# Graph layers: in the three weighted passes the weight table becomes the stationary operand and the features the moving one

## The chip, the cores and the metric

The kernel runs on one core of a Trainium2 chip. The metric is the device time of one launch in microseconds (us). The kernel before was timed three times: 2389.75, 2402.13 and 2397.53 us, median 2397.53 us.

## The reference, cut to what matters

A graph of 3125 nodes with 96 features and 103125 edges goes through four blocks. What this change touches is the second one, three GCN convolutions with edge weights:

```python
norm = dis[src_a] * w_a * dis[dst_a]
h = x @ W
msg = h[src_a] * norm[:, None]
out = jax.ops.segment_sum(msg, dst_a, num_segments=n)
return out + b
```

It is called three times, with a relu after the first and the second. After the third comes `layernorm(x + ...)`. The block before it (a mean over neighbours) and the one after it (two convolutions without weights, with a norm over the nodes) have the same shape of sum, with counts of edges in place of weights; an attention over the edges ends the network.

## The kernel before, in words

**Tables.** A first stage (`add_edges`) turns the list of edges into two dense tables of 3125 x 3125: how many edges go from one node to another (bf16) and the sum of their weights (f32). Each is stored in 25 blocks, one for each group of 125 target nodes (LANES = L = 125, NT = 25). A block holds 25 pieces of 125 source nodes x 125 target nodes.

**Passes and jobs.** `graph_layers` multiplies features by these tables. It has 6 passes (k = 0 to 5) of 25 jobs each, job j = 25 k + b making the sums of target group b. Passes 1, 2 and 3 are the weighted ones (`WEIGHTED`); they read `w_tab`, a ring of four slots of 1562.5 KB that SyncE's queue (SP) refills when the job four before it is done (`acc_done`). The other passes read the counts, `c_tab`, with the features split in three bf16 pieces side by side (288 columns).

**A job on TensorE.** In `main` (L1264) a job is 25 matmuls, t = 0 to 24, which add up in one PSUM bank, `acc[j % 2]`. In a count job the count block is stationary and the features stream (L1285): sums come out with the nodes on the partitions. In a weighted job the features of source group t, `g` (125 x 96), are stationary and the 125 x 125 piece of the weights streams (L1273): sums come out turned, 96 features on the partitions and 125 nodes in the free dimension. All of it is f32, and each f32 matmul shows as two instructions in the profile, with a weight load each.

**What follows a job.** The sums have to be multiplied by the layer's 96x96 weight, for which they must stand turned (features on partitions) in SBUF, in `aggT`. In a count job VectorE adds the three pieces into `h` (`sums`, L1390), TensorE turns `h` through `turn` (`turned`, L1225), and ScalarE copies the result into `aggT` (L1168). In a weighted job the sums are turned already, and ScalarE copies them from `acc` (L1165). Then TensorE makes the product (`product`, L1233), and VectorE ends the job (`finish`, L1434): scale, bias, relu, scale into the next pass's `g` (L1444, L1447), or in pass 3 the residual, a layer norm (`normalise`, L1418) and the split in bf16 pieces (L1453 to L1459). In pass 3 TensorE also turns x (`x_turn`, L1255) at place 21 of the following job.

**Order.** The order on each engine is written out by hand. TensorE puts the turn and the product of job j - 1 among the matmuls of job j, after matmul t = `at[0]` and t = `at[1]` (L1302). Where job j is weighted, that is (6, 10); after a weighted job there is only the product, at place 6. VectorE's loop over the weighted jobs (L1562) calls `finish(j)` and nothing else. `acc` has two banks: job j waits until the sums of job j - 2 have been read (L1290 to L1294). In the first job of a pass TensorE waits before each matmul for its piece of the last pass's result (`g_ready`, L1272; `g3_ready`, L1281).

Of the kernel before, what the change touches and what calls it, by code (L numbers as in the profile page):

```python
# [26 lines left out]
D = 96  # L27
# [3 lines left out]
NT = -(-N // P)  # L31
# [847 lines left out]
def graph_layers(nc, w_blocks, c_blocks, weights, rows, columns, kvq_w, kvq_b, kv_dram, q3_dram, ident, ci, x, eps, last_stored,  # L879
# [12 lines left out]
    with ctx:  # L892
# [120 lines left out]
        def c_index(j):  # L1013

            return j if j < NT else j - 3 * NT
# [96 lines left out]
        def _(act):  # L1112
# [45 lines left out]
            for k in range(PASSES):  # L1158
                for b in range(NT):
                    j = k * NT + b  # L1160
                    if k == 0:
                        own_rows(b)
                    if k in WEIGHTED:
                        act.wait_ge(acc_done, j + 1)
                        nc.scalar.copy(aggT[j % 2][0:D], acc[j % 2][0:D, 0:L]).then_inc(agg_ready, 1)  # L1165
                    else:
                        act.wait_ge(h_turned, c_index(j) + 1)
                        nc.scalar.copy(aggT[j % 2][0:D], turn[j % 2][0:D, 0:L]).then_inc(agg_ready, 1)  # L1168
                    if k == 0:
                        if b > 0:  # L1170
                            deviation(b - 1)
                        if b == W_DEG_AT:
                            act.wait_ge(dis_max, 1)
                            nc.scalar.activation(dis[:], dis[:], ACT.Sqrt).then_inc(dis_sqrt, 1)
                        if b > W_DEG_AT:
                            for late in range(min(5 * (b - W_DEG_AT - 1), b - 3), b - 2 if b == NT - 1 else min(5 * (b - W_DEG_AT), b - 2)):
                                first_g(late)
                        if b == NT - 1:
                            deviation(b)
                            for late in range(b - 2, NT):  # L1180
                                first_g(late)
                    elif k == 3:
                        act.wait_ge(var_ready, NT + b + 1)
                        nc.scalar.activation(sd[:], mv[:, 1:2], ACT.Sqrt, bias=eps[:, 0:1]).then_inc(sd_ready, 1)
                        act.wait_ge(x_turned, b + 1)
                        nc.scalar.copy(feat[1][:, nodes(b)], turn[j % 2][0:D, 0:L]).then_inc(feat_ready, 1)
                    elif k > 3:
                        act.wait_ge(prod_done, j + 1)
                        nc.scalar.copy(feat[k % 2][:, nodes(b)], prod[j % 2][0:D, 0:L]).then_inc(prod_copied, 1)
                if k > 3:  # L1190
                    i = k - 4
                    act.wait_ge(gvar_ready, i + 1)
                    nc.scalar.activation(gs[:, 1:2], gs[:, 0:1], ACT.Sqrt, bias=eps[0:D, 1:2]).then_inc(gsd_ready, 1)
                    act.wait_ge(gscale_ready, i + 1)

                    def relu(c):
                        area = slice(c * PB * L, (c + 1) * PB * L)
                        nc.scalar.activation(feat[k % 2][:, area], feat[k % 2][:, area], ACT.Relu, bias=gs[:, 4:5],
                                             scale=gs[:, 3:4]).then_inc(relu_ready, 1)

                    relu(0)
                    relu(1)
                    for c in range(CHUNKS):
                        if c + 2 < CHUNKS:
                            relu(c + 2)
                        if k == 4:
                            act.wait_ge(hT_turned, c + 1)
                            split(CHUNKS + c, turn[c % 2][0:L, 0:PB * D].rearrange("p (j d) -> p j d", d=D))
                            split_on(CHUNKS + c)
                        else:  # L1210
                            act.wait_ge(var5_ready, c + 1)
                            nc.scalar.activation(sd5[:], var5[:], ACT.Sqrt, bias=eps[:, 0:1]).then_inc(sd5_ready, 1)
                            act.wait_ge(shift5_ready, c + 1)
                            for u in range(PB):
                                done = nc.scalar.activation(x[0:L, PB * c + u, :], y5[c % 2][0:L, u, :], ACT.Identity,
                                                            bias=shift5[0:L, u:u + 1], scale=sd5[0:L, u:u + 1])
                            done.then_inc(out_ready, 1)
                            if c > 0:
                                out_copies(c - 1)
                            xT_copy(c)  # L1220
# [3 lines left out]
        def _(pe):  # L1224
            def turned(j):  # L1225

                if count_job(j):
                    pe.wait_ge(h_ready, c_index(j) + 1)
                    if 4 * NT <= j < 4 * NT + 2:
                        pe.wait_ge(feat_ready, NT - 1 + j % NT)  # L1230
                    nc.tensor.transpose(turn[j % 2][0:D, 0:L], h[j % 2][0:L, :], ident[0:L, 0:L]).then_inc(h_turned, 1)

            def product(j):  # L1233

# [29 lines left out]
            def main(j, t):  # L1264

                k, b = divmod(j, NT)
                if k in WEIGHTED:
# [2 lines left out]
                        pe.wait_ge(w_landed[s], 16 * (w_index(j) // W_SLOTS + 1))  # L1270
                    if b == 0:
                        pe.wait_ge(g_ready, (k - 1) * NT + t + 1)  # L1272
                    return nc.tensor.matmul(acc[j % 2][0:D, 0:L], g[(k - 1) % 2][0:L, t, :], w_tab[s][0:L, t, :], start=t == 0, stop=t == NT - 1)  # L1273
                s = c_index(j) % C_SLOTS
                if t == 0:
                    pe.wait_ge(c_landed[s], 16 * (c_index(j) // C_SLOTS + 1))
# [11 lines left out]
            for j in range(JOBS):  # L1288
                k, b = divmod(j, NT)
                if j >= 2:  # L1290
                    if count_job(j - 2):
                        pe.wait_ge(sums_read, c_index(j - 2) + 1)
                    else:
                        pe.wait_ge(agg_ready, j - 2 + 1)  # L1294
                for t in range(NT):
                    last = main(j, t)
                    if t == NT - 1:
# [1 line left out]
                    if j == W_DEG_AT and t == 23:  # L1299
                        pe.wait_ge(wsum_ready, W_SUM_PARTS)  # L1300
                        nc.tensor.transpose(deg[1][0:L, 0:NT], wsum[:], ident[0:NT, 0:NT]).then_inc(w_deg_ps, 1)
                    at = (6, 10) if not count_job(j) else (11, 19) if k == 0 else (8, 16)  # L1302
                    fresh = b == 0 and k in (4, 5)
                    if j >= 1 and not (b == 0 and k == 5):
                        if t == at[0] and count_job(j - 1):
                            turned(j - 1)
                        if t == at[1 if count_job(j - 1) else 0]:
                            product(j - 1)
                        if t == 21:
                            x_turn(j - 1)  # L1310
# [49 lines left out]
        def _(dve):  # L1360
# [29 lines left out]
            def sums(j):  # L1390

                b = j % NT
                dve.wait_ge(acc_done, j + 1)
                if c_index(j) >= 2:
                    dve.wait_ge(h_turned, c_index(j) - 1)
                pieces = acc[j % 2][0:L, 0:D3].rearrange("p (k c) -> p c k", k=3)
                if j < NT:
                    in_degree = acc[j % 2][0:L, D3:D3 + 1]
# [161 lines left out]
                    degrees()  # L1560
            finish(NT - 1)
            for j in range(NT, 4 * NT):  # L1562
                finish(j)
                dve.drain()
            for i in range(2):
                first = (4 + i) * NT
                sums(first)
# [1438 lines left out]
```

## Time and profile before

| | |
|---|---|
| median of three runs | 2397.53 us |
| span of the profiled execution | 2394.0 us |
| three weighted passes, 670 to 1090 us | 420 us, clock 1.00 |
| attention, from 1360 us on | 1034 us, clock 0.50 |

Of the profiled execution the profile has the span, first to last instruction; the median lies 3.5 us above it. PE is TensorE's matmuls, PEld its weight loads, DVE VectorE, ACT ScalarE, POOL GpSimd, SP the queue of SyncE. A row of a group gives the line, engine, operation, tiles (out<-in), shapes and count, then busy us and mean ns of one, then the idle time of the engine just before. `125*96 125x125` on a matmul says: stationary operand 125 rows x 96 columns, moving operand 125 x 125. A matmul's recorded duration holds its latency, so in a stream the distance between starts is shorter than the duration. The clock is the one granted to TensorE, 1.00 for 2.4 GHz and 0.50 for 1.2 GHz.

### The profile page before, as it was taken

Reading aid. Unit: us, or ns where it says so; the run is one execution under the profiler, and the core shown is the slowest. Engines: PE = TensorE matmul, PEld = TensorE weight load, DVE = VectorE, ACT = ScalarE, POOL = GpSimd, SP = SyncE. Lnnn points to the kernel's source line nnn. Section 1 sums busy time; section 2 is a strip of 40 time slices with the busy share of each in tenths; the row PEclk is TensorE's granted clock in tenths of the full one; section 3 lists DMA queues with packets and bytes.
Section 4 is the critical chain, followed back from the end, with each engine's and each line's share of the span. In section 5 each row is a group of like instructions: output and inputs, shape, how many; then the busy total and the mean of one; then the engine's idle time right before and its main releaser. Section 6 shows DMA issues by size and latency. Waiting matters only on the chain. (4 is left out here: it accounts for less than half of the span.)

```text
span 2394.0 us, 46888 instructions
## 1 busy us (share of the span) xinstructions
PE 1970.0 (82%) x14784; PEld 1716.6 (72%) x14785; DVE 1371.8 (57%) x3363; ACT 999.8 (42%) x2697; POOL 954.4 (40%) x947
## 2 busy tenths in 40 slices
PE   7888888887999999999898477777777777777775
PEld 3666666665799999998786367676767676776765
DVE  6999999997720111442324455555555555555554
ACT  5788888885320000111213334343434343434432
POOL 3122222222000000000001477777777777777775
PEclk9999999998999999999998555555555555555555
DMA  1477766768888887785562575565555555555552
GB/s 55 82 110 129 114 115 110 127 117 197 265 312 288 293 290 285 284 297 192 179 226 87 153 183 162 159 166 155 162 162 161 161 159 163 160 162 156 160 158 64
DMA packets 225379, 416.45 MB, mean 174 GB/s; under 512 B 130818, under 2 KB 150296, under 8 KB 215448
## 3 DMA queue, kind: packets, MB, share of 16 engines
q1 hardware_dynamic: 186414, 334.76, 50.1%
q0 software_dynamic: 38784, 79.48, 12.7%
q8 instruction: 88, 1.44, 0.2%
q14 instruction: 93, 0.76, 0.1%
HBM read 347.71 MB, written 66.43 MB: 173 GB/s over the span
## 5 line engine op out<-in xcount | busy, mean ns | idle before, releaser
L2354 POOL DMA_INDIRECT attention_windowed_vkv<-kv_dram,ttention_windowed_vsrc x808 | 781.1, 967 | 247.0 <-issue 222.5
L2445 PE MATMUL attention_windowed_vps_e<-attention_windowed_vwe,attention_windowed_vattr 97*128 97x96 f32 x1616 | 403.7, 431 | 119.9 <-DVE ttention_windowed_vscore L2520 90.7
L2459 PE MATMUL attention_windowed_vps_s<-attention_windowed_hot,attention_windowed_vmsg 128*104 128x32 f32 x1616 | 319.8, 362 | 177.4 <-DVE attention_windowed_vmsg L2524 153.4
L2445 PEld LDWEIGHTS attention_windowed_vps_e<-attention_windowed_vwe,attention_windowed_vattr 97*128 97x128 f32 x1616 | 366.5, 332 | 125.6 <-issue 125.6
L2459 PEld LDWEIGHTS attention_windowed_vps_s<-attention_windowed_hot,attention_windowed_vmsg 128*104 128x104 f32 x1616 | 297.4, 289 | 208.9 <-DVE attention_windowed_vmsg L2524 180.1
L1273 PE MATMUL graph_layers_acc<-graph_layers_w_tab,graph_layers_g 125*96 125x125 f32 x3750 | 417.8, 269 | 0.0
L678 ACT ACTIVATE add_edges_hot_lo<-add_edges_hot_lo,parts 128x128 bf16<-128x128 bf16 x1212 | 371.4, 387 | 90.1 <-DVE add_edges_hot_lo L761 90.1
L1273 PEld LDWEIGHTS graph_layers_acc<-graph_layers_w_tab,graph_layers_g 125*96 125x96 f32 x3750 | 406.6, 163 | 0.1
L729 PE MATMUL add_edges_ps_four<-add_edges_hot,add_edges_hot_lo 128*128 128x200 bf16 x2424 | 332.0, 258 | 0.0
L1103 POOL CAST graph_layers_g<-graph_layers_w_tab 125x480 bf16<-125x480 f32 x4 | 2.3, 585 | 736.0 <-ACT graph_layers_w_tab L1150 730.0
L2387 ACT ACTIVATE attention_windowed_vmsg<-ttention_windowed_vscore 128x32 f32<-128x32 f32 x202 | 46.3, 229 | 595.1 <-DVE ttention_windowed_vscore L2520 595.1
L2514 DVE TENSOR_TENSOR attention_windowed_vprod<-attention_windowed_vkv,attention_windowed_vps_q 128x384 f32<-128x384 f32 x202 | 111.5, 552 | 263.7 <-DMA attention_windowed_vkv<-kv_dram,ttention_windowed_vsrc 258.2
L797 DVE TENSOR_TENSOR strip<-strip,add_edges_ps_four 128x1000 f32 x202 | 239.9, 1187 | 23.7 <-PE add_edges_ps_four L729 22.8
L630 POOL MEMSET strip<- 128x500 f32 (+1 forms) x92 | 127.2, 1412 | 314.4 <-ACT add_edges_counts L668 235.8
L723 PE MATMUL add_edges_ps_four<-add_edges_hot,add_edges_hot_lo 128*128 128x200 bf16 x808 | 211.8, 262 | 0.0
L1285 PE MATMUL graph_layers_acc<-graph_layers_g,graph_layers_c_tab 125*128 125x288 bf16 (+1 forms) x1400 | 195.0, 289 | 0.7 <-DVE graph_layers_g L1459 0.7
L1444 DVE SCALAR_TENSOR_TENSOR graph_layers_z<-graph_layers_prod,graph_layers_dis,graph_layers_b 125x96 f32<-125x96 f32 x75 | 23.8, 318 | 298.1 <-PE graph_layers_prod L1253 298.1
L729 PEld LDWEIGHTS add_edges_ps_four<-add_edges_hot,add_edges_hot_lo 128*128 128x128 bf16 x2424 | 178.0, 99 | 1.1
L717 PE MATMUL add_edges_ps_four<-add_edges_noughts,add_edges_nought 1*128 1x500 bf16 x404 | 121.4, 380 | 64.0 <-DVE strip L797 63.7
L1285 PEld LDWEIGHTS graph_layers_acc<-graph_layers_g,graph_layers_c_tab 125*128 125x128 bf16 x1400 | 138.1, 99 | 34.9 <-DVE graph_layers_g L1459 1.0
L2382 ACT ACTIVATE attention_windowed_hot_T<-attention_windowed_far,attention_windowed_one 96x512 bf16<-96x512 f32 x202 | 145.8, 722 | 6.5
L2378 ACT ACTIVATE attention_windowed_far<-attention_windowed_vdrow,minus_node 96x512 f32<-96x512 f32 x202 | 142.6, 706 | 10.0 <-DMA ttention_windowed_q_rows<-q_dram 10.0
(244 smaller groups left out, 2458.0 us busy)
## 6 DMA issues: line engine op xcount, KB each, us to landing
graph_layers_w_tab<-w_blocks SPq DMA_DIRECT2D x75, 1562.5 KB
graph_layers_c_tab<-c_blocks SPq DMA_DIRECT2D x56, 800.0 KB
attention_windowed_vattr<-in_attr_T SPq DMA_DIRECT2D x202, 192.0 KB, 2.7
attention_windowed_vdrow<-dstf_dram SPq DMA_DIRECT2D x202, 192.0 KB, 3.2
w_blocks<-strip SPq DMA_DIRECT2D x24, 1562.5 KB, 13.9
c_blocks<-add_edges_counts SPq DMA_DIRECT2D x24, 800.0 KB, 4.8
first_table<-c_blocks SPq DMA_DIRECT2D x19, 800.0 KB, 4.3
attention_windowed_vkv<-kv_dram,ttention_windowed_vsrc POOLq DMA_INDIRECT x808
```

The lines of the kernel that those rows point to most:

```text
L630: nc.gpsimd.memset(strip[:, table, :, slot(b)][:, :, columns], 0.0).then_inc(done, 1)
L678: done = nc.scalar.activation(hot_lo[s][:, 1 + part, j, :], hot_lo[s][:, 0, j, :], ACT.Copy, scale=parts[:, part, bass.ds(g * G + j, 1)])
L723: nc.tensor.matmul(cells[:, 0], hot_lo[s][:, 0, e, :], hot[s][:, e, :], start=False, stop=m == Q4 - 1)
L729: last = nc.tensor.matmul(cells[:, 1], hot_lo[s][:, 1 + part, e, :], hot[s][:, e, :], start=False, stop=m == Q4 - 1 and part == 2)
L797: nc.vector.tensor_tensor(cells, cells, ps_four[u][:, :, 0:NT * REACH].rearrange("p c (t n) -> p c t n", n=REACH), ALU.add).then_inc(added, 1)
L1273: return nc.tensor.matmul(acc[j % 2][0:D, 0:L], g[(k - 1) % 2][0:L, t, :], w_tab[s][0:L, t, :], start=t == 0, stop=t == NT - 1)
L1285: return nc.tensor.matmul(acc[j % 2][:, 0:width], c_tab[s][0:L, t, :], g3[0:L, t, 0:width], start=t == 0, stop=t == NT - 1)
L2354: nc.gpsimd.indirect_dma_start(out=kv[s][:, k, :], out_offset=None, in_=kv_dram, in_offset=bass.IndirectOffsetOnAxis(ap=src4[s][:, k:k + 1 ...
L2378: nc.scalar.activation(far[s % 2][:], drow[:, s, :], ACT.Abs, bias=minus_node[0:Q_LANES, bass.ds(q, 1)]).then_inc(far_ready, 1)
L2382: nc.scalar.activation(hot_T[s][:].rearrange("p k e -> p (k e)"), far[s % 2][:], ACT.Relu, scale=-1.0, bias=one[0:Q_LANES]).then_inc(hot_T ...
L2445: nc.tensor.matmul(ps_e[s % BANKS][:, k, :], attr[:, s, k * P:(k + 1) * P], wes[:], start=True, stop=True)
L2459: last = nc.tensor.matmul(ps_s[s % 2], msg[s][:, k, :], hot[s][:, k, :], start=k == 0, stop=k == Q4 - 1)
```

## The change

In the weighted passes the operands change places: the piece of the weight table is stationary (125 columns) and the features stream (96 columns). The sums now come out by node, as in the count jobs. So each weighted job gets the same steps as a count job: VectorE copies `acc` into `h` (a plain copy in place of the sum of three pieces) and drains, TensorE turns `h`, ScalarE copies `turn` into `aggT`. TensorE's places in a weighted job become (3, 7). VectorE's loop calls `finish(j - 1)` and then `sums(j)`, and at the last job of a pass also `finish(j)`. All waits count all jobs now. In the first job of pass 4 (b = 0, a count job, places 8 and 16) the turn of job 99 stands at 8 and its product at 16, where before the product stood at 8. The turn of a job of pass 3 waits until the copy of x has left its `turn` bank.

```diff
@@ scalar
-                    if k in WEIGHTED:
-                        act.wait_ge(acc_done, j + 1)
-                        nc.scalar.copy(aggT[j % 2][0:D], acc[j % 2][0:D, 0:L]).then_inc(agg_ready, 1)
-                    else:
-                        act.wait_ge(h_turned, c_index(j) + 1)
-                        nc.scalar.copy(aggT[j % 2][0:D], turn[j % 2][0:D, 0:L]).then_inc(agg_ready, 1)
+                    act.wait_ge(h_turned, j + 1)
+                    nc.scalar.copy(aggT[j % 2][0:D], turn[j % 2][0:D, 0:L]).then_inc(agg_ready, 1)
@@ tensor
-                if count_job(j):
-                    pe.wait_ge(h_ready, c_index(j) + 1)
-                    if 4 * NT <= j < 4 * NT + 2:
-                        pe.wait_ge(feat_ready, NT - 1 + j % NT)
-                    nc.tensor.transpose(turn[j % 2][0:D, 0:L], h[j % 2][0:L, :], ident[0:L, 0:L]).then_inc(h_turned, 1)
+                pe.wait_ge(h_ready, j + 1)
+                if 3 * NT + 2 <= j < 4 * NT + 2:
+                    pe.wait_ge(feat_ready, j - 3 * NT - 1)
+                nc.tensor.transpose(turn[j % 2][0:D, 0:L], h[j % 2][0:L, :], ident[0:L, 0:L]).then_inc(h_turned, 1)
...
-                    return nc.tensor.matmul(acc[j % 2][0:D, 0:L], g[(k - 1) % 2][0:L, t, :], w_tab[s][0:L, t, :], start=t == 0, stop=t == NT - 1)
+                    return nc.tensor.matmul(acc[j % 2][0:L, 0:D], w_tab[s][0:L, t, :], g[(k - 1) % 2][0:L, t, :], start=t == 0, stop=t == NT - 1)
...
                 if j >= 2:
-                    if count_job(j - 2):
-                        pe.wait_ge(sums_read, c_index(j - 2) + 1)
-                    else:
-                        pe.wait_ge(agg_ready, j - 2 + 1)
+                    pe.wait_ge(sums_read, j - 1)
...
-                    at = (6, 10) if not count_job(j) else (11, 19) if k == 0 else (8, 16)
+                    at = (3, 7) if not count_job(j) else (11, 19) if k == 0 else (8, 16)
...
-                        if t == at[0] and count_job(j - 1):
+                        if t == at[0]:
                             turned(j - 1)
-                        if t == at[1 if count_job(j - 1) else 0]:
+                        if t == at[1]:
                             product(j - 1)
@@ vector
-                if c_index(j) >= 2:
-                    dve.wait_ge(h_turned, c_index(j) - 1)
+                if j >= 2:
+                    dve.wait_ge(h_turned, j - 1)
+                if not count_job(j):
+                    nc.vector.tensor_copy(h[j % 2][0:L], acc[j % 2][0:L, 0:D]).then_inc(sums_read, 1)
+                    dve.drain()
+                    dve.sem_inc(h_ready, 1)
+                    return
...
             for j in range(NT, 4 * NT):
-                finish(j)
-                dve.drain()
+                if j % NT > 0:
+                    finish(j - 1)
+                    dve.drain()
+                sums(j)
+                if j % NT == NT - 1:
+                    finish(j)
+                    dve.drain()
```

## Rows read from the trace of the kernel before

**Rows 1.** Busy time by stage: engines (instructions), clock, DMA share, GB/s.

```profile
588.00:670.00 82.00, 81.30 (x661) 65.03 (x659) 55.08 (x244) 27.47 (x108) 0.00 (x0) 1.00 0.87 289
670.00:1090.00 420.00, 420.00 (x3928) 419.88 (x3926) 91.33 (x355) 37.13 (x139) 0.00 (x0) 1.00 0.78 284
1360.00:2394.00 1034.00, 754.94 (x4059) 715.90 (x4057) 584.44 (x1612) 408.31 (x894) 771.75 (x799) 0.50 0.58 157
```

**Rows 2.** Groups by form, TensorE, whole span: busy us, mean ns, idle before.

```profile
L1273 PEld LDWEIGHTS graph_layers_acc<-graph_layers_w_tab,graph_layers_g 125*96 125x96 f32 x3750 | 406.6, 163 | 0.1
...
L1253 PEld LDWEIGHTS graph_layers_prod<-graph_layers_w,graph_layers_aggT 96*125 96x125 f32 x150 | 22.1, 187 | 0.0
...
L1273 PE MATMUL graph_layers_acc<-graph_layers_w_tab,graph_layers_g 125*96 125x125 f32 x3750 | 417.8, 269 | 0.0
...
L1253 PE MATMUL graph_layers_prod<-graph_layers_w,graph_layers_aggT 96*125 96x96 f32 x150 | 26.7, 259 | 0.0
```

**Rows 3.** Timeline, one job of pass 1: start us, length us, merged instructions.

```profile
799.82 0.29 PEld L1253 LDWEIGHTS graph_layers_prod<-graph_layers_w,graph_layers_aggT 96*125 96x125 f32 x2
799.92 0.36 PE L1253 MATMUL graph_layers_prod<-graph_layers_w,graph_layers_aggT 96*125 96x96 f32 x2
800.03 5.40 PEld L1273 LDWEIGHTS graph_layers_acc<-graph_layers_w_tab,graph_layers_g 125*96 125x96 f32 x50
800.12 5.53 PE L1273 MATMUL graph_layers_acc<-graph_layers_w_tab,graph_layers_g 125*96 125x125 f32 x50
...
804.18 0.26 ACT L1165 COPY graph_layers_aggT<-graph_layers_acc 96x125 f32<-96x125 f32 x1 [5.30 <-PE graph_layers_acc L1273]
805.38 0.29 PEld L1253 LDWEIGHTS graph_layers_prod<-graph_layers_w,graph_layers_aggT 96*125 96x125 f32 x2
```

**Rows 4.** Timeline, attention stage, runs of f32 matmuls.

```profile
1704.78 1.46 PEld L2459 LDWEIGHTS attention_windowed_vps_s<-attention_windowed_hot,attention_windowed_vmsg 128*104 128x104 f32 x8 [1.35 <-DVE attention_windowed_vmsg L2524]
...
1706.12 1.83 PEld L2445 LDWEIGHTS attention_windowed_vps_e<-attention_windowed_vwe,attention_windowed_vattr 97*128 97x128 f32 x8
1706.19 2.00 PE L2445 MATMUL attention_windowed_vps_e<-attention_windowed_vwe,attention_windowed_vattr 97*128 97x96 f32 x8
```

**Rows 5.** Groups by form, VectorE, whole span.

```profile
L1447 DVE TENSOR_SCALAR graph_layers_g<-graph_layers_z,graph_layers_dis 125x96 f32<-125x96 f32 x50 | 13.5, 270 | 4.8
...
L1440 DVE TENSOR_TENSOR graph_layers_y<-graph_layers_prod,x 125x96 f32<-125x96 f32 x25 | 6.3, 251 | 0.1
```

**Rows 6.** Timeline, one job of pass 3.

```profile
1000.93 0.29 PEld L1253 LDWEIGHTS graph_layers_prod<-graph_layers_w,graph_layers_aggT 96*125 96x125 f32 x2
...
1003.32 0.33 DVE L1432 TENSOR_SCALAR x<-graph_layers_y,graph_layers_mv,graph_layers_sd 125x96 f32<-125x96 f32 x1
...
1004.64 0.26 DVE L1459 TENSOR_TENSOR graph_layers_g<-graph_layers_z,graph_layers_g 125x96 bf16<-125x96 f32 x1
...
1005.40 0.26 ACT L1165 COPY graph_layers_aggT<-graph_layers_acc 96x125 f32<-96x125 f32 x1 [0.38 <-PE graph_layers_acc L1273]
```

**Rows 7.** Timeline, first job of pass 1.

```profile
670.12 1.57 PEld L1273 LDWEIGHTS graph_layers_acc<-graph_layers_w_tab,graph_layers_g 125*96 125x96 f32 x14
...
671.17 0.32 DVE L1406 SCALAR_TENSOR_TENSOR graph_layers_h<-graph_layers_z,graph_layers_cj,graph_layers_no_msg 125x96 f32<-125x96 f32 x1
...
671.63 0.12 PEld L1231 LDWEIGHTS graph_layers_turn<-ident,graph_layers_h 125*96 125x96 f32 x1
...
671.74 0.91 PEld L1273 LDWEIGHTS graph_layers_acc<-graph_layers_w_tab,graph_layers_g 125*96 125x96 f32 x8
```

**Rows 8.** Timeline, first job of pass 4.

```profile
1090.09 1.07 PEld L1285 LDWEIGHTS graph_layers_acc<-graph_layers_g,graph_layers_c_tab 125*128 125x128 bf16 x9
...
1091.19 0.31 PEld L1253 LDWEIGHTS graph_layers_prod<-graph_layers_w,graph_layers_aggT 96*125 96x125 f32 x2
...
1095.23 1.10 PEld L1285 LDWEIGHTS graph_layers_acc<-graph_layers_g,graph_layers_c_tab 125*128 125x128 bf16 x10 [1.00 <-DVE graph_layers_g L1459]
```

**Rows 9.** The page's first line.

```profile
span 2394.0 us, 46888 instructions
```

## The prediction

> **What bounds the kernel now.** I read the table of stages first [rows 1]. Between 670 and 1090 us lie the three weighted passes, and there TensorE (PE) is busy 420.00 of 420.00 us at granted clock 1.00, its weight loads (PEld) 419.88 us, while VectorE (DVE) and ScalarE (ACT) are busy 91 and 37 us and DMA 0.78. So in this stage nothing but TensorE's own stream sets the time, and work that DVE or ACT gets costs nothing as long as it is ready when TensorE comes to it. The groups by form [rows 2] say what the stream is: L1273 3750 times, which is 75 jobs x 25 blocks x 2, so one f32 matmul is two instructions, each with its own load. "Busy" overlaps here (3750 x 163 ns of loads are 611 us, yet 406.6 are counted), so durations are of no use and I take distances between starts.
>
> One job of the first weighted pass [rows 3]: the 50 matmuls after a product last 5.53 us, so (5.53 - 0.269)/49 = 107.4 ns from start to start. A job is 805.38 - 799.82 = 5.56 us; without 50 x 107.4 = 5.37 that leaves 0.195 for the two product instructions, 97.5 ns each. What fixes 107.4? Today's instruction streams 125 columns and loads 96. The attention stage has the other case, f32 loads of 128 columns with a stream of 96 at clock 0.50 [rows 1, 4]: loads follow each other every (1.83 - 0.332)/7 = 214 ns, and the loads of 104 columns every (1.46 - 0.289)/7 = 167 ns. That goes with the columns loaded, not with those streamed (96 and 32), and 214 ns at 1.2 GHz is 2.0 clocks a column. At 2.4 GHz that is 104.2 ns for 125 columns and 80 for 96. So today the stream of 125 columns is the longer side (104.2, and 3.2 more), and the load of 96 is hidden under it.
>
> **The change, part by part.**
>
> Main matmuls. Roles swap: 125 columns are loaded, 96 streamed. The stream falls to 80 ns, but the load rises to at least 104.2. The limit moves from one side to the other and stays about where it was. Nearest rows: the product (L1253) has exactly the new shape at full clock [rows 2, 3]. Its two loads start 22.1/75 us - 187 = 107 ns apart. That is one distance, and may still be held by the 125-column matmul ahead of it. Its two matmuls start 26.7/75 us - 259 = 97 ns apart, with one load already in hand. The long runs at the low clock give 214 x 125/128/2 = 104.3. Bounds: 97 below, and above 110: the first product load starts at 799.82 and its matmul at 799.92, 100 ns; the second matmul starts at 799.92 + 0.097 = 800.02 and the load after it at 800.03, 10 ns more. I take 107, the same shape at the same clock: 3750 x (107.0 - 107.4) = -1.5 us.
>
> Here a rule of the Trainium skill speaks against the change. "TensorE: Matmul & The Clock Gate", section "LDWEIGHTS (loading the stationary operand)", says that a load takes about columns/1.2 ns, whatever the rows. The trace agrees in slope: 187 against 163 ns for 125 against 96 columns at full clock [rows 2], 0.83 ns a column. By the page alone the unit would be 104, which is the first rival's. The same page, section "The mechanism", says that a load overlaps running matmuls only in other row groups. Then load and stream would add up to 184 ns in either order and the swap would cost nothing; the trace disagrees, since 107.4 is far less than 80 + 104.
>
> The turn. Every weighted job gets a transpose of h (L1231's form), 75 in all. Today's ones of this form cost one unit in the stream: load at 671.63, next load at 671.74 [rows 7]. 75 x 0.107 = +8.0 us, all on the path. Between 80 ns (the load of 96 columns sets it) and 107 each this is 6.0 to 8.0.
>
> The products. Today a product pair takes 97.5 ns an instruction, since hidden loads leave slack. In a stream bound by loads this is gone: 150 x (107 - 97.5) = +1.4 us (0 to 1.9).
>
> DVE's copy, ACT's copy. DVE gains 75 copies of 125x96 out of PSUM; the nearest operation with a PSUM source takes 251 ns [rows 5]. 19 us beside TensorE, covered if on time. ACT's copy is the same size (261 ns) and only has another source; it now waits for the turn, and behind it, in the third weighted pass (k = 3), stand the square root and the copy of x of that job, which come later anyway. Is h ready at its place? Times from a job's first load: the product stands 14 instructions in, so job start is 805.38 - 1.50 = 803.88, and ACT wakes at 804.18, +0.30 [rows 3]. DVE's copy then runs +0.30 to +0.55, the drain costs about 0.1 (4.8 us/50 ahead of L1447 [rows 5]), so h is ready at about +0.68. TensorE asks for it after 8 instructions, +0.86. Cover 0.18 us; if gone, every us late is paid 75 times, as the wait stands in front of all later matmuls of the job. The turn starts streaming at +0.97 and lasts 0.27, ACT copies +1.28 to +1.54, and the product comes after 17 instructions, +1.82. Cover 0.2 us.
>
> In the third weighted pass DVE has the long chain. From product load to the end of L1459 it is 1004.64 + 0.26 - 1000.93 = 3.97 us [rows 6]. The product moves from +1.50 to +1.82, so the chain ends at +5.79; the job lasts 54 instructions, 5.78, and the next copy may start at 5.78 + 0.30. Cover again 0.2 us. x (L1432) is ready at 1.82 + 2.72 = +4.54, its turn comes at +5.0. In the first two DVE has two operations a job, and is idle for most of it. SP's queue is released by the same acc_done, and DMA has a fifth of its time free [rows 1]. The new wait of job j for sums_read of j-2 was met a job earlier. g_ready for the first job of the next pass comes at about +3, wanted at +5.
>
> Two borders. First job after the counting pass: its turn moves from place 6 to 3, load at 670.12 + 0.86 = 670.98, but h is done at 671.17 + 0.32 = 671.49 [rows 7]. PE waits about 0.55 us there; the chain behind it keeps its time, and the wait of 0.1 us for the last g goes: +0.5 us. First job after the weighted passes: today the product stands after 9 bf16 matmuls at 1091.19, and the next thing to stall is block 24 at 1095.23, which waits for DVE's chain from that product [rows 8]. The turn now takes place 8 and the product place 16: 0.11 + 8 x 0.12 = +1.1 us, all of it on the path, since this chain ends last.
>
> Sum: -1.5 + 8.0 + 1.4 + 0.5 + 1.1 = +9.5 us. Of the profiled execution only its span, 2394.0 us [rows 9], is known; the median of the runs shown is 2397.5, the difference of 3.5 lying around the span. 2397.5 + 9.5 = 2407 us. The bound from which I call a change is 0.5%, 12 us, about what a measurement of this kernel can tell from none.
>
> **The rivals.**
>
> 1. The load is bare, 104.3 ns. For it: 2.0 clocks a column in the long runs at the low clock. Against: at full clock today's stream shows 3.2 ns over the bare number. Sum: 3750 x -3.1 = -11.6, turns +7.8, products +1.0, borders +1.6: -1.2 us, 2396.
>
> 2. Handover (slower). Each load waits for the matmul before it to start, and each matmul for most of its load, so that the two alternate. Place: each of the 3750 loads. At 110 ns: +9.8 + 8.2 + 1.9 + 1.6 = +21.5, 2419. It decides from a unit of 107.7 on (+12). For it: the 100 and 10 ns of the product pair. Against: the runs at low clock show nothing over the bare load.
>
> 3. A late h (slower). If copy, drain and semaphores take 0.28 us more than reckoned, 0.1 past the cover, that is 75 x 0.1 = +7.5 us over the forecast, 2414.5; from 0.03 us past the cover on the time passes the +12. For it: the place is 0.6 us earlier than today's first place. Against: the reckoning above.
>
> 4. The matmul sets the pace, as in the product pair, 97.5 ns: -37.1 + 7.3 + 0 + 1.6 = -28, 2369. Against: the load cadence in the attention stage.
>
> 5. The granted clock falls to its lower level in the passes. Unit about 209: 3750 x 0.101 = +380, near 2790. Against: TensorE keeps instructions without a gap, and the stage of bf16 matmuls before it holds 1.00 as well [rows 1]; the attention stage, with gaps, has 0.50.
>
> That the change doesn't do what it says I rule out: only operands and order change.
>
> **How the numbers follow.** Forecast (unit 105.5 to 108.5, covers hold) 0.50, with its own range 2401 to 2413; rival 1 0.23; rival 2 0.13; rival 3 0.06; rival 4 0.05; rival 5 0.03. Slower by over 0.5%: rivals 2, 3 and 5 are 0.22, and the forecast's upper part adds 0.16, 0.38. Faster: rival 4 and a little of rival 1, 0.06. Same 0.56. The range 2391 to 2425 takes in rivals 1 to 3 and leaves 4 and 5 out.
>
> **What would show it.** In the trace after: 50 matmuls of a job every 107 ns with loads back to back; the stage 8 us longer (428 instead of 420) at clock 1.00 with PE without idle time; 75 copies on DVE near 250 ns, and no wait of the turn for them but about 0.5 us at the first job; block 24 of the first job of pass 4 starting 6.2 us after its job's first load, where it is 1095.23 - 1090.09 = 5.1 now. Wrong would be a cadence under 105 or over 108, a turn that waits in every job, or a clock under 1.00 in the stage.

## The result and the profile after

| | median | runs |
|---|---|---|
| before, measured beside it | 2397.78 us | 4 |
| after | 2420.03 us | 4 |
| ratio, 95% interval | 1.009 | 1.0063 to 1.0118 |
| after once more, five rounds | 1.0072 | 1.0058 to 1.0086 |

The medians differ by 22 us in the first measurement and by 18 us in the second, 0.7 to 0.9%. Forecast was 2407 us, +9.5; the range of 2391 to 2425 holds the time. By the prediction's own bound of 0.5% the result counts as slower, to which it gave 0.38, and not as the same, to which it gave 0.56.

The stage of the weighted passes first, in the same view as [rows 1], then the page's first line, which answers to [rows 9].

```profile
672.00:1107.00 435.00, 434.70 (x4006) 434.43 (x4005) 110.77 (x431) 37.69 (x142) 0.00 (x0) 1.00 0.76 275
```

```profile
span 2417.4 us, 47286 instructions
```

TensorE is still busy all the time at clock 1.00, and DVE's busy share has grown from 0.22 to 0.25. The groups by form of this stretch (the line numbers have moved: L1273 is L1268, L1253 is L1248, L1231 is L1226) answer to [rows 2].

```profile
L1268 PE MATMUL graph_layers_acc<-graph_layers_g,graph_layers_w_tab 125*125 125x96 f32 x3750 | 430.0, 272 | 0.0
L1268 PEld LDWEIGHTS graph_layers_acc<-graph_layers_g,graph_layers_w_tab 125*125 125x125 f32 x3750 | 423.2, 189 | 0.0
...
L1389 DVE COPY graph_layers_h<-graph_layers_acc 125x96 f32<-125x96 f32 x75 | 19.3, 258 | 160.4 <-PE graph_layers_acc L1268 160.4
...
L1226 PEld LDWEIGHTS graph_layers_turn<-ident,graph_layers_h 125*96 125x96 f32 x81 | 12.2, 151 | 0.6 <-DVE graph_layers_h L1403 0.5
```

There is no idle time in front of the main matmuls, and 0.6 us in all in front of the turns. So nothing waits: the stream itself has become longer. One job of the first weighted pass shows it (compare [rows 3]).

```profile
801.82 0.30 PEld L1248 LDWEIGHTS graph_layers_prod<-graph_layers_w,graph_layers_aggT 96*125 96x125 f32 x2
...
802.04 4.67 PEld L1268 LDWEIGHTS graph_layers_acc<-graph_layers_g,graph_layers_w_tab 125*125 125x125 f32 x42
802.12 4.75 PE L1268 MATMUL graph_layers_acc<-graph_layers_g,graph_layers_w_tab 125*125 125x96 f32 x42
...
806.03 0.26 DVE L1389 COPY graph_layers_h<-graph_layers_acc 125x96 f32<-125x96 f32 x1 [3.03 <-PE graph_layers_acc L1268]
806.60 0.15 PEld L1226 LDWEIGHTS graph_layers_turn<-ident,graph_layers_h 125*96 125x96 f32 x1
806.71 0.95 PEld L1268 LDWEIGHTS graph_layers_acc<-graph_layers_g,graph_layers_w_tab 125*125 125x125 f32 x8
807.01 0.26 ACT L1164 COPY graph_layers_aggT<-graph_layers_turn 96x125 f32<-96x125 f32 x1 [5.50 <-PE graph_layers_turn L1226]
807.58 0.30 PEld L1248 LDWEIGHTS graph_layers_prod<-graph_layers_w,graph_layers_aggT 96*125 96x125 f32 x2
```

A job is 807.58 - 801.82 = 5.76 us, 0.20 more. The loads of the long run start (4.67 - 0.189)/41 = 109.3 ns apart, the turn takes 0.11, the product pair 0.22. From the first to the last load of L1268 it is 672.8 to 1107.1 us = 434.3, against 419.9 for L1273 (670.1 to 1090.0): +14.4 us.

The two borders, which answer to [rows 7, 8].

```profile
672.78 0.96 PEld L1268 LDWEIGHTS graph_layers_acc<-graph_layers_g,graph_layers_w_tab 125*125 125x125 f32 x8
...
674.20 0.12 PEld L1226 LDWEIGHTS graph_layers_turn<-ident,graph_layers_h 125*96 125x96 f32 x1 [0.46 <-DVE graph_layers_h L1403]
...
1107.18 1.07 PEld L1280 LDWEIGHTS graph_layers_acc<-graph_layers_g,graph_layers_c_tab 125*128 125x128 bf16 x9
...
1109.38 0.31 PEld L1248 LDWEIGHTS graph_layers_prod<-graph_layers_w,graph_layers_aggT 96*125 96x125 f32 x2
...
1112.84 0.26 DVE L1452 TENSOR_TENSOR graph_layers_z<-x,graph_layers_g 125x96 f32<-125x96 f32 x1 [0.43 <-issue]
...
1113.77 1.10 PEld L1280 LDWEIGHTS graph_layers_acc<-graph_layers_g,graph_layers_c_tab 125*128 125x128 bf16 x10 [1.35 <-DVE graph_layers_g L1456]
```

At the first the turn waits 0.46 us for h. At the last, the product comes 2.20 us after the first load instead of 1.10, and block 24 after 6.59 instead of 5.14, +1.45; 0.35 of that lies in one DVE instruction that was issued late, for nothing that the profile shows. It is late by the same 0.43 us in after_again and in border.

14.4 + 1.45 = 15.9 us are thus located. The span grew by 23.4. Of the other 7.5 us, 2.7 lie ahead of the stage, in code that the change leaves alone: the weighted passes begin at 670.1 in the one profile of before, at 672.8 in this one, and at anything from 664.8 to 686.9 in those of the experiments. The remaining 4.8 lie behind block 24 of the last border. From the last load of the stage to the end of the span it is 1304.0 us in before and 1310.3 here, and anything from 1304.0 to 1312.0 over all kernels; no experiment takes this part apart.

### The profile page after: what moved, and what is told of

The parts are those of the page before. It is cut to its first block and busy times, and to the rows that moved or that the text cites. A ratio compares the mean times of both kernels' runs of the same rounds, so it can differ in the third digit from the quotient of the medians.

```text
span 2417.4 us, 47286 instructions
## 1 busy us (share of the span) xinstructions
PE 1992.7 (82%) x14859; PEld 1736.5 (72%) x14860; DVE 1392.8 (58%) x3438; ACT 999.9 (41%) x2697; POOL 956.1 (40%) x947
## 5 line engine op out<-in xcount | busy, mean ns | idle before, releaser
L1268 PE MATMUL graph_layers_acc<-graph_layers_g,graph_layers_w_tab 125*125 125x96 f32 x3750 | 430.0, 272 | 0.0
L1268 PEld LDWEIGHTS graph_layers_acc<-graph_layers_g,graph_layers_w_tab 125*125 125x125 f32 x3750 | 423.2, 189 | 0.0
L1164 ACT COPY graph_layers_aggT<-graph_layers_turn 96x125 f32<-96x125 f32 x150 | 39.2, 261 | 432.1 <-PE graph_layers_turn L1226 432.1
L724 PE MATMUL add_edges_ps_odeg<-add_edges_hot_hi,add_edges_hot_lo 128*128 128x26 bf16 x808 | 147.0, 182 | 0.0
```

The source lines that it names most:

```text
L724: last = nc.tensor.matmul(ps_odeg[:], hot_lo[s][:, 0, e, :], hot_hi[s][:, e, :], start=isinstance(g, int) and g == 0 and e == 0, stop=is_l ...
L1268: return nc.tensor.matmul(acc[j % 2][0:L, 0:D], w_tab[s][0:L, t, :], g[(k - 1) % 2][0:L, t, :], start=t == 0, stop=t == NT - 1)
```

## The experiments

"Stage" is the time from the first to the last load of the weighted matmuls.

| kernel | stage us | job, pass 1 | against before (95%) |
|---|---|---|---|
| before | 419.9 | 5.56 | 1 |
| after | 434.3 | 5.76 | 1.009 (1.0063 to 1.0118) |
| swap_alone | 427.8 | 5.67 | 1.0036 (1.0018 to 1.0055) |
| turn_alone | 427.8 | 5.67 | 1.0037 (1.0021 to 1.0054) |
| places_6_10 | 436.8 | 5.76 | 1.0113 (1.0086 to 1.014) |
| no_table_dma | 434.3 | 5.76 | 1.010 (1.0068 to 1.0131) |
| three_copies | 438.9 | 5.82 | 1.0091 (1.0069 to 1.0114) |
| stream_80 | 433.0 | 5.75 | one run |
| stream_48 (ratio: stream_48_again) | 822.3, clock 0.50 | 11.0 | 1.1696 (1.158 to 1.1812) |
| load_96 | 360.1 | 4.57 | one run |
| border | 434.3 | 5.76 | one run |
| after_again | 434.3 | 5.76 | 1.0072 (1.0058 to 1.0086) |
| wide_250 | 413.8 | 5.48 | 0.9973 (0.9962 to 0.9985) |

**The operands alone.** One line of before is changed.

```diff
-nc.tensor.matmul(acc[j % 2][0:D, 0:L], g[(k - 1) % 2][0:L, t, :], w_tab[s][0:L, t, :], ...)
+nc.tensor.matmul(acc[j % 2][0:L, 0:D], w_tab[s][0:L, t, :], g[(k - 1) % 2][0:L, t, :], ...)
```

> The kernel before with the two operands of the weighted matmuls exchanged and nothing else: no turn, no copy on VectorE, ScalarE still copies 96 partitions x 125 columns out of acc (sums not turned, so the layer's values are not the reference's). Theory (the pace is the load of 125 columns): the matmuls of a job start 109 ns apart instead of 107.4, the product pair 110 each, so a job is 52 x 109 = 5.67 us instead of 5.56 and the stage about 427 to 428 us, +7 to +8; ratio about 1.003. Rival (the turn and the late h carry it all, the swap is free): 107.4 ns, 420 us, ratio 1.000. Rival (handover grows when h is not waited for): over 112 ns, stage over 437.

Its timeline:

```profile
800.48 0.30 PEld L1253 LDWEIGHTS graph_layers_prod<-graph_layers_w,graph_layers_aggT 96*125 96x125 f32 x2
800.70 5.54 PEld L1273 LDWEIGHTS graph_layers_acc<-graph_layers_g,graph_layers_w_tab 125*125 125x125 f32 x50
806.15 0.30 PEld L1253 LDWEIGHTS graph_layers_prod<-graph_layers_w,graph_layers_aggT 96*125 96x125 f32 x2
```

(5.54 - 0.189)/49 = 109.2 ns, a job of 5.67 us, stage +7.9. With no turn and no wait for h in it, the exchange alone costs half of the stage's loss. That the swap is free is refuted. The sums of this kernel are not the reference's, as the layer's weight meets them unturned; its main matmuls are those of the changed kernel.

**The turn alone.** A transpose of a constant, in before's order of operands.

```diff
+                    if t == 3 and not count_job(j):
+                        nc.tensor.transpose(deg[1][0:D, 0:L], ident[0:L, 0:D], ident[0:L, 0:L])
```

> The kernel before with one more transpose a weighted job at place 3, of a constant, whose result nobody reads: the turn's cost on TensorE by itself. Theory: one unit a job, 75 x 0.107 = +8.0 us, stage 428, ratio 1.003. Rival (the short load of a transpose lets it slip in): 75 x 0.05 = +4 us or less. Together with the swap alone this has to give the +14.4 us of the stage that the changed kernel shows; if the two add to clearly less, a wait for h is in it.

```profile
801.29 0.12 PEld L1303 LDWEIGHTS graph_layers_deg<-ident 125*96 125x96 f32 x1
801.40 0.70 PEld L1273 LDWEIGHTS graph_layers_acc<-graph_layers_w_tab,graph_layers_g 125*96 125x96 f32 x6
...
806.96 0.12 PEld L1303 LDWEIGHTS graph_layers_deg<-ident 125*96 125x96 f32 x1
```

Transpose to transpose 5.67 us, 0.11 more than before, stage +7.9. 7.9 + 7.9 = 15.8 against 14.4 for both: no wait for h is hidden in the stage's +14.4. The turn is even cheaper in the changed kernel. In swap_alone a job of 5.67 us less 50 x 109.2 ns leaves 0.21 for the product pair; in after 5.76 less 50 x 109.3 leaves 0.295 for pair and turn, so 0.085 for the turn instead of 0.11. A turn loads 96 columns and streams 125; 85 ns is also what a load of 96 columns costs in load_96 below.

**Later places.** The only edit to after is

```diff
-                    at = (3, 7) if not count_job(j) else (11, 19) if k == 0 else (8, 16)
+                    at = (6, 10) if not count_job(j) else (11, 19) if k == 0 else (8, 16)
```

> The changed kernel with the turn at place 6 and the product at place 10, the places of the count jobs before: h has 0.65 us more. Theory (h is in time at place 3, with 0.15 to 0.2 us over): job stays 5.76 us in passes 1 and 2; the wait of 0.5 us at the first weighted job goes, -0.5 us. In pass 3 the product comes 0.65 us later, VectorE's chain ends after the next job's sums, and h is then late by up to 0.3 us but the place is later too: no wait. Stage 434 us as in the changed kernel, within 1. Rival (a late h is in the 14 us): the stage falls by 75 times the wait, to 430 or less.

Passes 1 and 2 keep 5.76 us a job, so h is in time at place 3. But the stage is 436.8, and I missed the reason beforehand. The last pass by stage, after and then this kernel, and the job's turn of x in this one:

```profile
962.00:1107.10 145.10, 145.10 (x1344) 145.10 (x1343) 65.51 (x266) 19.84 (x73) 0.00 (x0) 1.00 0.73 267
```

```profile
969.50:1117.10 147.60, 147.60 (x1340) 145.72 (x1340) 65.03 (x264) 19.85 (x73) 0.00 (x0) 1.00 0.72 262
...
1044.97 0.12 PEld L1257 LDWEIGHTS graph_layers_turn<-ident,x 125*96 125x96 f32 x1
```

The turn of x stands at place 21 whatever the product does. With the product 0.65 us later, x is finished later than place 21, and TensorE waits 0.1 us a job, +2.5 us in the pass (the loads are busy 145.72 of 147.60 us, where in after they have no gap). My expectation, 434 within 1, missed this. The cover that counts in this pass is x, not h. The places (3, 7) of the change are the better ones.

**No table traffic.**

```diff
                     if n >= W_SLOTS:
-                        sp.wait_ge(acc_done, j - W_SLOTS + 1)
+                        return
...
-                        pe.wait_ge(w_landed[s], 16 * (w_index(j) // W_SLOTS + 1))
+                        pe.wait_ge(w_landed[s], 16)
```

> The changed kernel in which only the first four blocks of the weight table are loaded and then used by all 75 jobs (the other 71 loads are left out, values differ): no DMA beside the weighted passes. Theory (109 ns is the weight load's own time): pace stays 109 ns, stage 434 us. Rival (loads through the weight port lose time to the DMA writes into the table, 280 GB/s): the pace falls to 107.4 or below, stage 428 or less.

```profile
799.92 4.67 PEld L1268 LDWEIGHTS graph_layers_acc<-graph_layers_g,graph_layers_w_tab 125*125 125x125 f32 x42
...
805.68 4.67 PEld L1268 LDWEIGHTS graph_layers_acc<-graph_layers_g,graph_layers_w_tab 125*125 125x125 f32 x42
```

The same 4.67 us for 42 loads, the same 434.3 us. Traffic into the table, 275 GB/s in after and next to none here, does not slow its loads.

**Fewer columns streamed.** `acc[..][0:L, 0:48]` and `g[..][0:L, t, 0:48]` in after, then the same with 80.

> The changed kernel with half of the features streamed: 48 instead of 96 columns over the same loads of 125 (the other half of the sums is left out). Theory (the load of 125 columns sets 109 ns alone): starts stay 109 ns apart, stage 434 us. Rival (load and stream share the time in part, the rest over 104 comes from the stream): the distance falls with the columns, to 105 or less, stage under 420. Full serial work (109 = part of 104 + part of 80) would give well under 90.

> The changed kernel with 80 of 96 feature columns streamed over the same loads of 125 (the other 16 are left out of the sums). With 48 the clock fell to its lower level in the weighted passes, so the question on the pace at full clock stayed open. Theory (the load alone sets 109 ns): where the clock holds 1.00 the starts stay 109 ns apart and the stage 434 us. Rival (the stream has a part in 109): about 105 and 420. If the clock falls here too, the stage is near 820 us and the pace 210 ns.

> The kernel with 48 columns streamed once more, timed in one round. Theory (the fall of the clock belongs to the narrow stream): granted clock 0.50 in the weighted passes again, about 2800 us. Rival (a chance state of that one execution): clock 1.00, stage 434 us or less, about 2412 us.

The narrow one went another way than either theory. Its stages (columns as in [rows 1]), of the first execution and then of the second:

```profile
668.00:676.00 8.00, 7.66 (x69) 7.11 (x68) 4.70 (x21) 5.85 (x22) 0.00 (x0) 1.00 0.86 362
676.00:684.00 8.00, 8.00 (x42) 8.00 (x41) 0.85 (x3) 0.26 (x1) 0.00 (x0) 0.51 0.58 207
...
680.00:1480.00 800.00, 800.00 (x3870) 800.00 (x3869) 104.33 (x402) 31.26 (x117) 0.00 (x0) 0.50 0.41 146
```

```profile
680.00:1480.00 800.00, 800.00 (x3878) 800.00 (x3877) 103.95 (x401) 31.71 (x119) 0.00 (x0) 0.50 0.40 146
```

Some microseconds into the weighted passes the granted clock falls to its lower level and stays there for all three, in both executions (stages of 822.3 and 817.0 us). PE and PEld show 8.00 of 8.00 us busy all along, so neither row warns of it; the only edit was a stream of 48 columns beside loads of 125. Why that lowers the clock is not shown. At 80 columns the clock stays, and the question on the pace is answered:

```profile
680.00:1090.00 410.00, 410.00 (x3792) 410.00 (x3791) 99.38 (x382) 30.12 (x113) 0.00 (x0) 1.00 0.78 281
...
800.74 4.67 PEld L1268 LDWEIGHTS graph_layers_acc<-graph_layers_g,graph_layers_w_tab 125*125 125x125 f32 x42
800.82 4.74 PE L1268 MATMUL graph_layers_acc<-graph_layers_g,graph_layers_w_tab 125*125 125x80 f32 x42
```

109.3 ns again with a sixth of the stream gone. The load sets the pace, and the stream has no part in it.

**Fewer columns loaded.** After, with `w_tab[s][0:L, t, 0:D]` and 96 rows of sums.

> The changed kernel with 96 instead of 125 columns of each weight piece loaded, 96 streamed (29 of 125 targets of each block left out). Theory (a f32 load costs 2 clocks a column and about 5 ns): 80 + 5 = 85 ns, a job 50 x 85 + 0.11 + 0.2 = 4.6 us, stage near 345 us unless VectorE's chain of pass 3 (4.0 us after a product) or the table's DMA (0.77 of 5.76 us a block, 4.4 us) then stands in front. Handover (a fixed 28 ns or more that does not overlap, whichever side is longer): over 100 ns.

```profile
799.79 3.65 PEld L1268 LDWEIGHTS graph_layers_acc<-graph_layers_g,graph_layers_w_tab 125*96 125x96 f32 x42
799.88 3.73 PE L1268 MATMUL graph_layers_acc<-graph_layers_g,graph_layers_w_tab 125*96 125x96 f32 x42
```

(3.65 - 0.165)/41 = 85.0 ns: 80 of columns and 5 more, as 109.3 is 104.2 and 5. The fixed cost of handing over of 28 ns or more that my expectation named is refuted. A job is 4.57 us, as expected; the stage is 360 rather than 345, since in the third pass DVE's chain no longer fits in a job: there the turn waits for h in 23 jobs, 9.2 us in all.

**DVE three times as slow.**

```diff
+                    nc.vector.tensor_copy(no_msg[0][0:L], acc[j % 2][0:L, 0:D])
+                    nc.vector.tensor_copy(no_msg[1][0:L], acc[j % 2][0:L, 0:D])
                     nc.vector.tensor_copy(h[j % 2][0:L], acc[j % 2][0:L, 0:D]).then_inc(sums_read, 1)
```

> The changed kernel with VectorE's copy of the sums made three times (two into tiles nobody reads), h ready 0.45 to 0.5 us later. Theory (in the changed kernel h is ready about 0.2 us before TensorE asks): the wait is 0.25 to 0.3 us in each of 75 jobs, +19 to +22 us over the changed kernel, stage 453 to 456, ratio 1.017. Rival (VectorE's work here is free, at a busy share of a quarter): stage 434, ratio 1.009. Rival (h was the pace already): 75 x 0.5 = +37 us.

```profile
799.87 4.67 PEld L1268 LDWEIGHTS graph_layers_acc<-graph_layers_g,graph_layers_w_tab 125*125 125x125 f32 x42
...
803.86 0.26 DVE L1389 COPY graph_layers_no_msg<-graph_layers_acc 125x96 f32<-125x96 f32 x1 [3.03 <-PE graph_layers_acc L1268]
804.04 0.25 DVE L1390 COPY graph_layers_no_msg<-graph_layers_acc 125x96 f32<-125x96 f32 x1
804.20 0.25 DVE L1391 COPY graph_layers_h<-graph_layers_acc 125x96 f32<-125x96 f32 x1
804.55 0.12 PEld L1226 LDWEIGHTS graph_layers_turn<-ident,graph_layers_h 125*96 125x96 f32 x1
804.55 0.99 PEld L1268 LDWEIGHTS graph_layers_acc<-graph_layers_g,graph_layers_w_tab 125*125 125x125 f32 x8
...
805.47 0.30 PEld L1248 LDWEIGHTS graph_layers_prod<-graph_layers_w,graph_layers_aggT 96*125 96x125 f32 x2
```

A miss in size. Independent copies start 0.16 to 0.18 us apart, not 0.25, so h comes 0.34 us later and not 0.5. Job 5.82 us, +0.06, stage +4.6 us over after. From the last copy's end at 804.45 to the turn's load it is 0.10 us. In after that would have allowed the turn at 806.29 + 0.10 = 806.39, and it stands at 806.60: cover 0.21 us, as reckoned (0.18). So 0.34 - 0.21 = 0.13 us of wait should show. It does: from the first load of the 42 to the turn's it is 4.68 us instead of 4.56. But half of it comes back at once. The load behind the turn starts at the same 804.55 instead of 0.11 us later, and from the turn's load to the product's it is 0.92 us instead of 0.98. So 0.12 - 0.06 = 0.06 us a job is left, which is the stage's 4.6 us in 75 jobs. A wait of this length for h costs half of itself.

**The last border.** After, with places (3, 7) also in the first job of pass 4.

> The changed kernel with the places (3, 7) also in the first job of pass 4, instead of (8, 16). Theory: the product comes 9 bf16 matmuls earlier, about 1.0 us, the turn waits some 0.15 us for h; from that job's first load to its block 24 it is 5.6 us instead of 6.6. Nothing else moves. Rival (block 24 waits for something else): 6.6 us stays.

```profile
1110.56 0.45 PEld L1280 LDWEIGHTS graph_layers_acc<-graph_layers_g,graph_layers_c_tab 125*128 125x128 bf16 x4
...
1111.23 0.12 PEld L1226 LDWEIGHTS graph_layers_turn<-ident,graph_layers_h 125*96 125x96 f32 x1 [0.21 <-DVEq L1390]
...
1116.26 1.10 PEld L1280 LDWEIGHTS graph_layers_acc<-graph_layers_g,graph_layers_c_tab 125*128 125x128 bf16 x10 [1.35 <-DVE graph_layers_g L1456]
```

5.70 us from the first load to block 24, with a wait of 0.21 us for h: 0.89 of the 1.45 us belonged to the product's place. In what is left, 0.56, the product comes 1.33 us after the first load instead of before's 1.10, and the DVE instruction is 0.35 us late. One microsecond doesn't show in the time (2423.48 us, one run).

**After once more.**

> The changed kernel once more, unchanged, in five rounds. Theory: of the first measurement's +22 us some 16 are the stage (+14.4) and its last border (+1.5), the rest is spread between executions in the table-building stage ahead; more rounds bring the ratio to 1.007, 1.0055 to 1.0085, and the stage itself is 434.3 again within 0.5. Rival (the change also slows a later or an earlier stage by 5 us): 1.009 to 1.010 stays.

2412.75 against 2394.73 us, 1.0072, and the stage is 664.8 to 1099.1 = 434.3 us again. The interval, 14 to 21 us, holds the 15.9 us located in the profile. This profile shows one thing more, behind the wait for block 24. The 3.6 us from there on, here and then in after (columns as in [rows 1]):

```profile
1105.80:1109.40 3.60, 3.58 (x18) 2.51 (x19) 0.46 (x1) 0.26 (x1) 0.00 (x0) 0.59 0.59 204
```

```profile
1113.80:1117.40 3.60, 3.60 (x30) 2.97 (x31) 0.46 (x1) 0.52 (x2) 0.00 (x0) 1.00 0.62 203
```

The granted clock drops for some 3.4 us, and TensorE makes 18 matmuls instead of 30. At this place the drop is in the profiles of after_again, no_table_dma, three_copies, places_6_10 and load_96, and not in those of after and stream_80, all with the later product; it is in none of before, swap_alone, turn_alone, wide_250 and border, where the product comes earlier and the idle time at this border is shorter. The first matmul of L1348 (L1340 in the changed kernel) comes 89.0 us after the stage's last load in before, 90.4 in after, 91.8 in after_again and 89.6 in border. So the last border costs 1.4 us, or 2.8 where the clock drops. That the longer idle time brings the drop is the likely reading; no experiment tests it alone.

**One load for two pieces.** Before, with `w_tab[s][0:L, t:t + 2, :]` streamed at even t.

> The kernel before with one load of the features for two pieces of the table: 12 matmuls of 250 streamed columns and one of 125 a job in place of 25 of 125 (odd pieces are multiplied with the wrong features, so the sums differ). It asks what the kernel before could still gain by sharing a load. Theory (a stream costs 2 clocks a column and about 3 ns an instruction): 24 x 211.5 + 2 x 107.4 + 0.195 = 5.49 us a job instead of 5.56, stage 414, -6 us, ratio 0.9975. Rival (the gap is proportional to the columns): 420, ratio 1.000. Rival (loads in the way today): over 10 us gained.

0.9973: about 6 us less, a job of 5.48 us. So an instruction whose stream is the longer side costs 2 clocks a column and 3 ns, and these 3 ns are all that sharing a load could win. The odd pieces are multiplied with the wrong features here; a kernel with the right sums was not built.

## Why the prediction was right or wrong

**What bounds the stage** was right: TensorE's stream, which the change moves from the stream's side to the load's side (swap_alone, stream_80, load_96).

**The signs of being wrong.** The prediction named a cadence over 108 ns as one, and it is 109.3: by its own test the part on the main matmuls failed, though the time lies in its range. It also forecast a stage of 428 us (434.3) and block 24 after 6.2 us (6.59). The range held because it was wide enough for rival 2, whose price came; the mechanism behind the forecast was right and its largest term was not.

**Main matmuls: the term that was mis-sized.** I took 107.0 ns and -1.5 us. Measured are 109.3, which is +1.9 x 3750 = +7.1 us. The step that failed is "I take 107, the same shape at the same clock": the two loads of a product pair are one distance in a stream bound by matmuls, and I had written myself that it may be held by the matmul ahead. That distance was misread, too: 22.1/75 us - 187 is 107.7, not 107, which alone would have made the term +1.1 and the sum +12, on the bound itself; and the single load records of these passes lie 105 to 106 ns apart. The row could not decide it. The long runs at the low clock gave the columns' part right (104.3) and hid the fixed part. The 3.2 ns beside the old stream's 104.2 told that there is one at full clock; for a load it is 5.

**Rival 2** named the price, 110 ns and 2419 us, nearly as it came (109.3; 2420 and 2412.75), for a reason that load_96 does not bear out: with 85 ns from load to load no 100 ns from load to matmul can lie in series. That rival 2's number was so near is luck. Whether the 5 ns are the load's own or a handover of that size, these runs do not tell. **Rival 1** (bare loads, 104.3) and **rival 4** (97.5) are out by swap_alone.

**The turn**, +8.0: +7.9 by itself, 75 x 0.085 = +6.4 us in the changed kernel, within the bounds given (6.0 to 8.0). **The products**, +1.4: the pair went from 0.195 to 0.21 us, +1.1. **Borders**, +0.5 and +1.1: 0.46 us of waiting, less the 0.1 that went, and +1.45, of which 0.89 by the product's place (border), or more where the clock drops behind it. 7.1 + 6.4 + 1.1 + 0.4 is 15.0, and the stage grew by 14.4; readings to 10 ns a job leave 0.75 us in 75 jobs open.

**Covers held.** h was in time with 0.21 us over (0.18 reckoned), the passes without idle time. **Rival 3** was real as a mechanism, at three copies, but not in the change, and there it cost half of the wait. In the third pass I gave x half a microsecond (+4.54 to +5.0); places_6_10 shows that 0.65 us later is 0.1 too late.

**Rival 5** did not come, but I excluded it for a reason that is wrong: "TensorE keeps instructions without a gap". Its second reason, that the bf16 stage ahead holds 1.00, says nothing of a narrower stream. stream_48 keeps them without a gap too and ran its passes at 0.50. The Trainium skill ("TensorE: Matmul & The Clock Gate", section "What's actually happening") says that the clock follows how busy the engine has been; by its busy rows here TensorE was busy throughout, so these rows are not what tells.

**The rule against the change** ("LDWEIGHTS (loading the stationary operand)" of the same page of the Trainium skill): 24.3 ns for 29 columns between load_96 and after is 0.84 ns a column, which agrees with its 1/1.2. Its formula has no fixed part, and at the measured 5 ns an instruction it is 19 us short over 3750.

**The chances.** I gave 0.38 to slower by over 0.5%, 0.56 to no change. With 109.3 in place of 107 the same sum is +9.5 + 8.6 = +18 us, and with the cheaper turn 16.5. The threshold lay at a unit of 107.7, and the row from which 107.0 was taken could not tell it from 107.7; the forecast stood too near to the bound to favour either side of it.

## What to carry to other kernels

Before exchanging stationary and moving operand, ask which of load and stream is longer, each with its columns and its own fixed cost: here, at full clock, f32 streams cost 2 clocks a column + 3 ns an instruction (125 and 250 columns), loads 2 clocks + 5 ns (96 and 125), and the longer one counts alone. An exchange that keeps the longer side's columns wins nothing on the matmuls, however much shorter the other side becomes, and each step added to restore the layout is paid on a saturated engine (a turn cost 0.085 to 0.11 us a job). Where an engine issues thousands of equal instructions, take the pace from a long run bound by the same side and at the same clock, since 2 ns each, over 3750, are 7 us here.

## What the runs showed that was not expected

- A stream of 48 columns beside f32 loads of 125 brought the granted clock from 1.00 to 0.50 some microseconds into the passes and kept it there to the end of the passes, over 800 us, in both executions, with PE and PEld busy without a gap. With 80 and with 96 columns it stayed 1.00. Halving the streamed work made the stage 388 us longer.
- A longer idle time of TensorE at one border (2.00 and 1.35 us in after_again) was followed by a drop of the clock for 3.4 us in five of the seven such profiles whose passes ran at 1.00, and in none of the five with the shorter one.
- A wait of 0.12 us for a turn's operand cost 0.06: the load behind it was ready to follow without its usual distance.
- Three independent VectorE copies of 125x96 out of PSUM, recorded at 0.25 us each, start 0.16 to 0.18 us apart.
- Table traffic of 275 GB/s into the very tile that is loaded as weights costs the loads nothing measurable: 4.67 us for 42 with and without it.
- The profiled executions of all these kernels differ by up to 22 us in when the code ahead of the stage, which is the same in all, is done (664.8 to 686.9 us); the length of the stage repeats to 0.1 us (434.3 in after, after_again, no_table_dma and border).
